# From the third tile on, x, z and h are transposed by DMA on SP's queue instead of by TensorE and ScalarE

## What is computed

```python
x = x + xattn(layernorm(x), ctx)     # both sides scaled by 128-wide blocks, rounded to fp8
                                     # values; einsum over 512; 4 batches of 512 x 512
z = layernorm(x)
probs = softmax(z @ w_router)        # 128 experts, the top 4 weigh mixtures of 8 bases
basis = silu(z @ w_gate) * (z @ w_up)        # 512 -> 8 * 256
mixed = sum over the top 4 of weight * mix[expert] @ basis      # 256 wide
shared = silu(z @ s_gate) * (z @ s_up)                          # 512 wide
x = x + mixed @ w_down + shared @ s_down
```

## Time and profile before

| | |
|---|---|
| median of 3 runs | 653.34 us |
| the profiled execution, its own time | 653.38 us |
| its span in the profile | 651.6 us |
| TensorE busy | 559.2 us, 86% |
| VectorE, ScalarE, POOL busy | 395.2, 287.9, 198.2 us |
| bytes moved by the DMA engines | 25.47 MB |

### The profile page before, as it was taken

The page is one execution under the profiler, slowest core; times in us unless marked ns, Lnnn a source line. Parts: engine busy times, 40 slices in busy tenths (PEclk is TensorE's granted clock), DMA queues, the critical chain, the costliest instruction groups (busy, mean ns, idle before and its releaser), DMA issues.

```text
span 651.6 us, 8729 instructions
## 1 busy us (share of the span) xinstructions
PE 559.2 (86%) x2978; PEld 273.3 (42%) x2993; DVE 395.2 (61%) x1133; ACT 287.9 (44%) x413; POOL 198.2 (30%) x242
## 2 busy tenths in 40 slices
PE   0306646589999999999999999999999999999995
PEld 0103213244444454444454545444544444444442
DVE  6946567377867657584847476857565655553312
ACT  4366537535344444444444443443635353534311
POOL 3301021313744231644441413463514131312110
PEclk9999657699999999999999999999999999999997
DMA  8421430201010200010100200000100010000000
GB/s 296 148 72 64 162 129 6 74 1 34 2 33 1 98 2 33 1 33 2 32 1 26 73 21 13 2 31 2 33 2 33 1 33 1 17 1 17 2 17 16
DMA packets 13852, 25.47 MB, mean 39 GB/s; under 512 B 1264, under 2 KB 1776, under 8 KB 13808
## 3 DMA queue, kind: packets, MB, share of 16 engines
q1 hardware_dynamic: 13808, 24.92, 11.3%
HBM read 20.72 MB, written 4.19 MB: 38 GB/s over the span
## 4 chain that ended last, share of the span: by engine, by line
PE 75%; DVE 9%; ACT 8%; issue 5%; POOL 1%; DMA 1%; another core or an unknown queue 1%; SPq 0%; POOLq 0%; DVEq 0%; ACTq 0%
PE gate L871 30%; PE up L871 28%; PE even L913 9%; PE turn L884 2%; PE odd L853 2%; ACT gate_up_hi L559 2%; ACT gate_up_hi L572 1%; DVE x L1115 1%; DVE gate_up_lo L1283 1%; ACT L618 1%; PE turn L840 1%; DMA ctx_in<-in_ctx 1%; PE odd L829 1%; DVE ctx_m L1037 1%
## 5 line engine op out<-in xcount | busy, mean ns | idle before, releaser
L871 PE MATMUL gate<-gate_up_hi,zT_hi 128*128 128x512 f16 x320 | 125.1, 391 | 0.0
L871 PE MATMUL gate<-gate_up_lo,zT_hi 128*128 128x512 f16 x320 | 125.0, 391 | 0.0
L871 PE MATMUL gate<-gate_up_hi,zT_lo 128*128 128x512 f16 x320 | 124.6, 389 | 0.0
L871 PE MATMUL up<-gate_up_hi,zT_hi 128*128 128x512 f16 x320 | 121.3, 379 | 0.8
L871 PE MATMUL up<-gate_up_lo,zT_hi 128*128 128x512 f16 x320 | 121.3, 379 | 0.0
L871 PE MATMUL up<-gate_up_hi,zT_lo 128*128 128x512 f16 x320 | 121.3, 379 | 0.0
L634 ACT ACTIVATE silu<-gate,w_back 128x512 f32<-128x512 f32 x80 | 55.0, 688 | 92.1 <-PE gate L871 91.9
L1211 DVE SCALAR_TENSOR_TENSOR part<-up,coef,silu 128x256 f32<-128x256 f32 x128 | 55.9, 479 | 55.7 <-PE up L871 55.2
L506 POOL TENSOR_TENSOR hid<-hid,part 128x256 f32<-128x256 f32 x48 | 34.8, 725 | 168.7 <-DVE part L1211 168.6
L490 POOL TENSOR_TENSOR gain<-var,minus_half 128x1 f32<-128x1 f32 x16 | 11.3, 703 | 151.6 <-DVE neg_mean L1129 151.6
L871 PEld LDWEIGHTS gate<-gate_up_hi,zT_lo 128*128 128x128 f16 x320 | 32.1, 100 | 40.2 <-issue 4.3
(11 more groups left out here) (162 smaller groups left out, 931.6 us busy)
## 6 DMA issues: line engine op xcount, KB each, us to landing
ctx_in<-in_ctx SPq DMA_DIRECT2D x16, 256.0 KB, 3.7
x_in<-in_x SPq DMA_DIRECT2D x16, 256.0 KB, 2.8
out<-y_out SPq DMA_DIRECT2D x16, 256.0 KB, 2.0
stage<-in_L_ffn_w_up SPq DMA_DIRECT2D x3, 1024.0 KB, 5.0
stage<-in_L_ffn_w_gate SPq DMA_DIRECT2D x2, 1024.0 KB, 7.6
ctx_in<-in_L_ffn_w_gate SPq DMA_DIRECT2D x2, 1024.0 KB, 5.1
stage<-in_L_ffn_shared_w_gate SPq DMA_DIRECT2D x1, 1024.0 KB, 8.2
stage<-in_L_ffn_shared_w_up SPq DMA_DIRECT2D x1, 1024.0 KB, 9.2
```

The source lines that it names most:

```text
L871: mm = nc.tensor.matmul(ps[:], zT[a][:, t % 2, kc, :], wgu[w][:, n - 1 + i, kc, :], start=(m == 0), stop=(m == 3 * KC - 1))
```

## The change

For tiles from the third on (z for `t >= 2`, x for `t >= 3`) and for h of all tiles, SP issues a DMA transpose from SBUF to SBUF into the same buffers. `turn_x`, `turn_z` and `turn_h` leave TensorE's program (the first two stay for the first tiles), `keep_x`, `keep_z` and `keep_h` leave ScalarE's; readers and writers wait on the DMA's semaphores in place of `kept` and `turned`. The core of the diff:

```diff
@@ def uses0 / uses1: the lists of what uses the two PSUM banks
-                out += [("coef", t), ("h", t - 1)] + [("ctx", c) for c in early]
-                out += [("z", t + 1)] * front + [("ctx", c) for c in late] + [("weight", t + 1)] * front
-            return out + [("h", TILES - 1)]
+                out += [("coef", t)] + [("ctx", c) for c in early]
+                out += [("ctx", c) for c in late] + [("weight", t + 1)] * front
+            return out
...
@@ block.sync
+            def turn_h(s):
+
+                wait_at(sp, down_full, s)
+                sp.wait_ge(h_hi_done, s + 1)
+                sp.dma_start_transpose(hT[HI][:], hs[HI][:]).then_inc(hT_in[HI], 16)
+                sp.wait_ge(hid_step, HID_STEPS * (s + 1))
+                sp.dma_start_transpose(hT[LO][:], hs[LO][:]).then_inc(hT_in[LO], 16)
+
+            def turn_z(t):
+
+                sp.wait_ge(up_full, use(t - 2, PAIRS - 1) + 1)
+                sp.wait_ge(z_hi_done, t + 1)
+                sp.dma_start_transpose(zT[HI][:, t % 2], z[HI][:]).then_inc(zT_in[HI], 16)
+                sp.wait_ge(ln_step, LN_STEPS * (t + 1))
+                sp.dma_start_transpose(zT[LO][:, t % 2], z[LO][:]).then_inc(zT_in[LO], 16)
+
+            def turn_x(t):
+
+                sp.wait_ge(att_full, KC * t)
+                sp.wait_ge(x_round, X_ROUNDS * (t + 1))
+                sp.dma_start_transpose(x_qT[:], x_q[:]).then_inc(xT_in, 16)
...
                 if t >= 1:
+                    turn_h(t - 1)
                     store(t - 1)
+                if 2 <= t + 1 < TILES:
+                    turn_z(t + 1)
+                if 3 <= t + 2 < TILES:
+                    turn_x(t + 2)
+            turn_h(TILES - 1)
             store(TILES - 1)
...
@@ block.scalar, the loop over t
-                if front:
-                    keep_x(t + 1)
+                if t == 1:
+                    keep_x(2)
                 silus(t, -1)
                 h_hi(t - 1)
-                keep_h(t - 1, HI)
                 silus(t, 0)
-                keep_h(t - 1, LO)
...
-                if front:
-                    keep_z(t + 1)
...
             h_hi(TILES - 1)
-            keep_h(TILES - 1, HI)
-            keep_h(TILES - 1, LO)
...
@@ block.tensor, down(t)
                     if w == 0:
-                        pe.wait_ge((kept0, kept1)[a], turn_of(a, "h", t) + 1)
+                        pe.wait_ge(hT_in[a], 16 * (t + 1))
...
@@ block.tensor, the loop over t
-                if front:
-                    pair(t, -1, {0: lambda: coefs(t), 2: lambda: turn_x(u), 6: lambda: attend(u, 0), 7: lambda: attend(u, 1)})
+                if t == 1:
+                    pair(t, -1, {0: lambda: coefs(t), 2: lambda: turn_x(2), 6: lambda: attend(u, 0), 7: lambda: attend(u, 1)})
+                elif front:
+                    pair(t, -1, {0: lambda: coefs(t), 6: lambda: attend(u, 0), 7: lambda: attend(u, 1)})
...
-                pair(t, 0, {1: lambda: turn_h(s, HI), 2: lambda: attend(u, 2), 3: lambda: turn_h(s, LO),
-                            6: lambda: attend(u, 3)} if front else
-                           {1: lambda: turn_h(s, HI), 3: lambda: turn_h(s, LO)})
+                pair(t, 0, {2: lambda: attend(u, 2), 6: lambda: attend(u, 3)} if front else {})
                 down(s)
...
-                second = {1: lambda: turn_z(u, HI), 2: lambda: turn_z(u, LO), 6: lambda: route(u)} if front else {}
+                second = {6: lambda: route(u)} if front else {}
...
-            turn_h(TILES - 1, HI)
-            turn_h(TILES - 1, LO)
             down(TILES - 1)
```

More of the change, by code:

```diff
@@ L240, in build @@
         turned0, kept0, turned1, kept1 = sem("turned0"), sem("kept0"), sem("turned1"), sem("kept1")
+        hT_in = [sem("hT_hi_in"), sem("hT_lo_in")]
+        xT_in = sem("xT_in")
+        zT_in = [sem("zT_hi_in"), sem("zT_lo_in")]
         y_done, y2_done = sem("y_done"), sem("y2_done")
@@ L308, in uses1 @@
                 front, first = t + 1 < TILES, lane("ctx", 1) if t == 1 else []
-                out += [("x", t + 1)] * front + [("h", t - 1)] + first[:1] + [("z", t + 1)] * front + first[1:]
+                out += [("x", 2)] * (t == 1) + first
                 if ctx_lanes_in(t):
                     out += lane("ctx", t // NB + 1)
-            return out + [("h", TILES - 1)]
+            return out
         USES = [uses0(), uses1()]
-        TURNS = [[use for use in uses if use[0] in ("ctx", "x", "z", "h")] for uses in USES]
+        TURNS = [[use for use in uses if use[0] in ("ctx", "x", "z")] for uses in USES]
         def turn_of(bank, kind, i):
@@ L356, in wait_ctx_rounded, with wait_z_turned @@
                 eng.wait_ge(ctx_round_pool, CTX_ROUNDS * (c + 1 if c < 2 else c - 1))
+        def wait_z_turned(eng, t, h):
+            if t >= 2:
+                eng.wait_ge(zT_in[h], 16 * (t - 1))
+            else:
+                eng.wait_ge((turned0, turned1)[h], turn_of(h, "z", t) + 1)
         block = stack.enter_context(nc.Block())
@@ L482, in round_x @@
                 if t >= 1:
-                    pool.wait_ge(turned1, turn_of(LO, "x", t - 1) + 1)
+                    if t >= 4:
+                        pool.wait_ge(xT_in, 16 * (t - 3))
+                    else:
+                        pool.wait_ge(turned1, turn_of(LO, "x", t - 1) + 1)
                 ch.did(nc.gpsimd.tensor_tensor(x_q[:], x_v[:], x_m[:], ALU.subtract))
@@ L606, in norm2 @@
                 if t >= 1:
-                    act.wait_ge(turned0, turn_of(HI, "z", t - 1) + 1)
+                    wait_z_turned(act, t - 1, HI)
                 nc.scalar.activation(z[0][:], x2[:, t % 3, :], ACT.Identity, bias=shift2[:], scale=gain2[:]
@@ L644, in h_hi @@
                 act.wait_ge(hid_step, HID_STEPS * t + 5)
-                if t >= 1:
-                    act.wait_ge(turned0, turn_of(HI, "h", t - 1) + 1)
+                wait_at(act, hT_in[HI], 16 * t)
                 nc.scalar.activation(hs[0][:], hid[:, t % 2, :], ACT.Copy, scale=hid_scale[:]
                                      ).then_inc(h_hi_done, 1)
[L650 to L654, removed]
             norm1(0)
@@ L820, in attend @@
                 if kc == 0:
-                    pe.wait_ge(kept1, turn_of(LO, "x", t) + 1)
+                    if t >= 3:
+                        pe.wait_ge(xT_in, 16 * (t - 2))
+                    else:
+                        pe.wait_ge(kept1, turn_of(LO, "x", t) + 1)
                     pe.wait_ge(kept0, turn_of(HI, "ctx", t // NB * NB + NB - 1) + 1)
@@ L844, in route @@
             def route(t):
-                pe.wait_ge(kept0, turn_of(HI, "z", t) + 1)
-                pe.wait_ge(kept1, turn_of(LO, "z", t) + 1)
+                if t >= 2:
+                    pe.wait_ge(zT_in[HI], 16 * (t - 1))
+                    pe.wait_ge(zT_in[LO], 16 * (t - 1))
+                else:
+                    pe.wait_ge(kept0, turn_of(HI, "z", t) + 1)
+                    pe.wait_ge(kept1, turn_of(LO, "z", t) + 1)
                 if t == 0:
@@ L874, in pair @@
                     mm.then_inc(full, 1)
[L876 to L886, removed]
             def turn_weight(t):
@@ L1135, in z_lo @@
                 if t >= 1:
-                    dve.wait_ge(turned1, turn_of(LO, "z", t - 1) + 1)
+                    wait_z_turned(dve, t - 1, LO)
                 ch.did(nc.vector.tensor_tensor(z[1][:], y2[:], z[0][:], ALU.subtract))
@@ L1236, in split_h @@
                 ch.sync()
-                if t >= 1:
-                    dve.wait_ge(turned1, turn_of(LO, "h", t - 1) + 1)
+                wait_at(dve, hT_in[LO], 16 * t)
                 ch.did(nc.vector.scalar_tensor_tensor(hs[1][:], hid[:, t % 2, :], hid_scale[:], hs[0][:],
```

## The result

The changed kernel takes 634.85 us (median of 4 runs, 634.54 to 636.88) against 653.18 us (652.23 to 653.42) for the kernel before on the same chip: a ratio of 0.9728, 95% interval 0.9706 to 0.9751. The forecast was 635.2 us and 0.972. The profiled execution has a span of 632.8 us against 651.6.

What follows compares the result with a forecast made beforehand. TensorE was taken as the bound for the 15 tiles after the ramp. 653.4 us less 20.1 leaving TensorE plus 1.9 in the tail gave 635.2 us, ratio 0.972; range for 8 in 10 from 631.5 to 655.

Steps and rivals of the forecast that it cites:

- What leaves TensorE: Slots of the h, z and x transposes in the tiles, plus two early waits for `hs_hi`: 20.06 us saved.
- fourth rival: No change: waits on POOL or VectorE replace the saving, needing 1.3 us in each tile; 653 us, chance 0.04.
- ScalarE's copies at nothing: The removed copies `keep_h`, `keep_z` and `keep_x`, some 0.6 to 0.8 us each, were priced at no gain.
- The price of a transpose: DMA transpose of h on SP's queue: 3.0 us taken, between 2.0 and 6.1; z and x somewhat less.
- the bound's picture of the pieces: Upper bound: h transpose as 768 pieces of 256 B, 48 per DMA engine at 85 ns each, giving 6.1 us.
- The cover: Time from `hs_hi` to its reader `down`: 6.6 us in the middle tile, 4.2 in tile 1, about 4.5 in tile 2.
- rivals 2 and 3: `down` waits for serial h transposes: 640 to 652 us, chance 0.14; or slower, from 5.1 us per transpose, chance 0.20.
- The tail: After the last `pair`, `down` starts 1.2 us later and the clock returns 5 us after that; costs 1.9 us.

Runs made afterwards that it cites:

- ghost_turns: Changed kernel with as many identity transposes put back on TensorE as the change removed; 652.42 us, ratio 1.0000 to the kernel before.
- ghost_copies: Changed kernel with a ScalarE copy of the old size at each place the change took one from; 635.90 us, ratio 0.9752 to the kernel before.
- ahead3: Changed kernel with 3 junk DMA transposes of `hs_hi` on SP's queue ahead of the real one; 648.18 us, ratio 0.9926 to the kernel before.
- ahead5: Changed kernel with 5 junk DMA transposes of `hs_hi` on SP's queue ahead of the real one; 703.98 us, ratio 1.0762 to the kernel before.
- ctx_dma: Changed kernel with the context's 12 transposes of batches 1 to 3 by DMA on SP's queue too; 626.64 us, ratio 0.9586 to the kernel before.
- ctx_dma_tail_pe: Changed kernel with the context's 12 transposes by DMA too and the last tile's h turned by TensorE; 625.45 us, ratio 0.9573 to the kernel before.
- h_only: Kernel before with only h's transposes by DMA, x and z still on TensorE and ScalarE; 645.70 us, ratio 0.9895 to the kernel before.

## Why the prediction was right

The forecast was 635.2 us and the measured 634.85. Its steps:

- **What leaves TensorE: right in kind, 1.7 us too much.** The sum was 20.06 us, the loop gave 18.38. The middle tile gave 1.34 us (32.9 to 31.56) where 1.36 was written. ghost_turns shows that from tile 2 on it is slots and nothing else. Short fell tiles with work on the context, t = 5, 8 and 9: the distances from `down` to `down` shrank there by 0.8 to 0.9 us, 1.5 us less than three times 1.36. TensorE then meets VectorE's attention sums 0.36 and 0.37 us early, ahead of `down`, and the router's weights 0.39 us early:

```profile
308.70 1.47 PE L936 MATMUL even<-down_hi,hT_hi 128*128 128x512 f16 x6 [0.37 <-DVE x L1136]
...
439.14 1.04 PE L936 MATMUL even<-down_hi,hT_hi 128*128 128x512 f16 x4 [0.36 <-DVE x L1136]
```

  These are new waits of the fourth rival's kind, in few tiles. Tile 1 has one more, 0.22 us at `attend`, and tile 4 gave 0.3 us more than forecast, as a wait of 0.28 us for the router's weights went. The prediction allowed for new waits only in tile 2, and there it was right: the wait for `ctx_q` grew from 1.56 to 2.00 us by the 0.46 us of z.
- **ScalarE's copies at nothing: right**, shown by ghost_copies.
- **The price of a transpose: right.** 3.0 us for h was taken between 2.0 and 6.1; it is 2.7. Right with it the bound's picture of the pieces: the queue has 47904 more packets under 512 B than before, of which 45568 are the 256 B pieces of 32 h and 41 z and x transposes (768 and 512 each) and the rest 32 for each of the 73. But 85 ns is not what such a piece costs: the 256 B packets took 21 ns each on average. The prediction had said that they would cost much less, and used 85 ns for its upper bound. The rule of the Trainium skill that was weighed ("Advanced Engine Details and Errata", X-Bar Transpose (TRN2)) calls transposes as fast as regular DMAs. Measured are 2.7 against 2.1 us, and 1.21 against 0.48 us of SP. The same page's DGE: Hardware vs Software rates the hardware path as less efficient for transposes than the software path; no run here issues one that way, so that stays untested. Neither mattered behind 6.6 us of cover.
- **The cover: right.** 6.6 us in the middle, 4.5 in tiles 1 and 2 (predicted 4.2 and 4.5), no wait for a DMA in the loop. ahead3 puts the edge where the prediction put it. The break-even of rivals 2 and 3 was not tried, and it left the clock out: in ahead5 that made 16.8 of 66.74 us, so slower transposes would have hurt more than was worked out.
- **The tail: the DMA's part right, the clock's part wrong.** 1.2 us were forecast for the later start and 1.07 measured; 0.7 us for a longer half-clock stretch, and the last down took 0.09 us more. (Worked out again, this part is 0.9 us: the 650.3 lacks the 0.2 us until the result is read, which the 648.4 holds. The forecast would then be 635.4.) The second six matmuls take 1.82 us (626.17 to 627.99), so the clock returned within them, some 3.5 us after TensorE began again and not 5. The step assumed that the clock comes back a fixed time after TensorE starts again; in the traces above it rose 2.9 us (ctx_dma) to 5.7 us (ctx_dma_tail_pe) after TensorE's first instruction behind the wait, and the last down takes 4.76 to 6.60 us. That the clock's part came out small in this run is luck: in h_only, with the same tail, the last down took 6.46 us. The tail came to 1.16 us instead of 1.9.

The loop was 1.7 us short and the tail 0.7 us better. The ramp, which the change does not touch, was 1.68 us shorter in this profile (`coefs` of tile 1 at 129.99 against 131.67), 1.1 of it from its first loads. In the other runs it lies anywhere from 129.8 to 132.7. The profiled execution's gain of 18.8 us is these three: 18.38 less 1.16 and 1.68 more. That the total fits to 0.35 us is therefore partly luck; the stages fit to 1.7 and 0.7 us.

## What to carry to other kernels

Where TensorE is busy for 100% of a stretch, as in the middle tiles here, a transpose on it costs the distance by which it pushes the next matmul back (0.33 us for six here, not 0.22 each), and moving it to the DMA engines gives back that and, in this kernel, nothing for the engine that copied. Read the cover from the timeline, from the producer's end to the reader's start with the moved work taken out, and compare it with 2.4 to 2.9 us for a transpose of 128 to 192 KB and 1.2 to 1.3 us of the queue for each. A transpose whose copy waits in another engine's in-order queue can hold more than itself, so look for the waits behind that queue: here the context's 12 transposes were worth 9.4 us where their slots are worth 2.8.

## What the runs showed of the hardware

- A DMA transpose holds SP for about the same time whether it moves 128 or 192 KB (medians of 1.19 to 1.26 us in the changed kernel, single ones up to 2.2), a plain DMA of 192 KB for 0.48 us.
- Transposes in a row hold it for 1.29 us each in most cases (3.87 us for three in ahead3, 6.55 us for five in ahead5), and the last lands 2.9 us after issue.
- The transposes' packets of 256 B took 21 ns each on average, those of 2048 B 96 ns.
- A wait of 3.78 us of TensorE left the granted clock at 1.00 (ahead5), and waits of 2.48 us (ahead3) and 3.49 us (ahead5) were followed by stretches at 0.50. The wait's length alone did not decide it.
- An idle time in a row of TensorE understates what the wait cost by 0.16 us, the matmul's 0.38 us less the pitch of 0.216 us.
- After an idle time of 4.6 to 7.6 us the last down, the same 18 matmuls, took from 4.76 to 6.60 us, and 4.08 us with TensorE kept at work.
